# The front of the two routed feed-forward layers: fewer identity products, statistics first, a third chunk copied inside the attention step, more tiles normalised on ScalarE

## The reference, cut to what matters

```python
x = x + 0.5 * L0_ffn(layernorm(x))   # 8 experts, the best 2 of a softmax gate, and a shared expert with a sigmoid gate
x = x + L0_attn(layernorm(x))        # 16 heads of width 8, 4 key heads
x = x + 0.5 * L0_ffn(layernorm(x))
x = x + 0.5 * L1_ffn(layernorm(x))   # 8 zones, 3 of them by the pooled sequence
x = x + L1_attn(layernorm(x))
x = x + 0.5 * L1_ffn(layernorm(x))
```

```python
logits = x_flat @ gate_w.T
scores = softmax(logits)
_, topk_ids = lax.top_k(scores, 2)
w = scores * one_hot(topk_ids, 8).sum(axis=1)
```

## Time and profile before

| what | value |
|---|---|
| runs, median of 3 | 1454.32 us (1452.37 to 1456.07) |
| the profiled execution, its own time | 1451.83 us |
| its span | 1450.0 us |
| TensorE busy | 1394.0 us, 96% of the span |
| VectorE, ScalarE, GpSimd busy | 1129.6, 976.5, 640.3 us |
| first expert product of stage 0 | 38.9 us after the start |
| first expert product of stage 2 | 619.7 us after the start |

### The profile page before, as it was taken

The page is one execution under the profiler, slowest core; times in us unless marked ns, Lnnn a source line. Parts: engine busy times, 40 slices in busy tenths (PEclk is TensorE's granted clock), DMA queues, the critical chain, the costliest instruction groups (busy, mean ns, idle before and its releaser), DMA issues.

```text
span 1450.0 us, 26990 instructions
## 1 busy us (share of the span) xinstructions
PE 1394.0 (96%) x9348; PEld 1116.9 (77%) x9348; DVE 1129.6 (78%) x2503; ACT 976.5 (67%) x1759; POOL 640.3 (44%) x600
## 2 busy tenths in 40 slices
PE   6999999999999999999999999999989999989998
PEld 6788888766666665678888878999967777769998
DVE  6787777688988889678777787787788889855765
ACT  5666666557777777766666668877656666658886
POOL 6466666610000000146666667677512323356664
PEclk9999999999999999999999999999999999989999
DMA  6000000000000000002000011000000000000001
GB/s 184 1 1 1 1 1 1 1 1 1 1 1 1 1 1 2 1 1 90 1 1 1 1 38 51 1 2 2 1 1 2 1 2 2 2 1 2 15 16 30
DMA packets 13318, 16.84 MB, mean 12 GB/s; under 512 B 768, under 2 KB 10496, under 8 KB 12928
## 3 DMA queue, kind: packets, MB, share of 16 engines
q1 hardware_dynamic: 13184, 15.11, 3.4%
HBM read 13.01 MB, written 2.10 MB: 10 GB/s over the span
## 4 chain that ended last, share of the span: by engine, by line
PE 82%; DVE 10%; issue 3%; ACT 2%; POOL 2%; DMA 0%; POOLq 0%; SPq 0%; DVEq 0%; ACTq 0%
PE PS L852 19%; PE PS L879 9%; PE PS L2073 9%; PE PS L2090 8%; PE PS L1017 5%; PE PS L1037 5%; PE PS L1025 4%; PE PS L996 2%; PE PS L1414 2%; PE PS L1439 2%; PE PS L1448 2%; PE PS L1424 1%; PE PS L170 1%; PE PS L1472 1%; PE PS L1396 1%
## 5 line engine op out<-in xcount | busy, mean ns | idle before, releaser
L759 POOL TENSOR_TENSOR RR<-AR,RR 128x512 fp32r<-128x512 f32 x150 | 193.9, 1293 | 139.4 <-ACT RR L784 133.0
L823 ACT ACTIVATE AR<-PS 128x512 f32<-128x512 f32 x224 | 134.0, 598 | 148.4 <-PE PS L852 144.7
L724 DVE TENSOR_TENSOR AR<-AR,PS 128x512 f32<-128x512 f32 x224 | 153.4, 685 | 101.4 <-PE PS L852 90.3
L1142 ACT ACTIVATE AR<-PS 128x512 f32<-128x512 f32 x256 | 152.5, 604 | 85.6 <-PE PS L1025 84.8
L1222 DVE TENSOR_REDUCE AR<-PS 128x2 f32<-128x512 f32 x256 | 172.5, 687 | 21.5 <-PE PS L1017 20.6
L852 PE MATMUL PS<-XHI,WG 128*128 128x512 f32 x448 | 178.7, 399 | 0.4 <-DVE XLO L459 0.3
L852 PE MATMUL PS<-XHI,WU 128*128 128x512 f32 x448 | 175.0, 391 | 2.0 <-DVE AR L724 2.0
L730 DVE TENSOR_TENSOR AR<-AR,PS 128x512 f32<-128x512 f32 x224 | 154.0, 687 | 9.4 <-PE PS L868 1.3
L2345 POOL CAST SL<-ZW 128x1024 fp32r x96 | 100.3, 1045 | 84.3 <-PE PS L2090 83.8
L2073 PE MATMUL PS<-XHI,SL 128*128 128x256 f32 x576 | 134.1, 288 | 2.2 <-DVE XTR L2240 1.9
L2168 ACT ACTIVATE PS<-PS 128x1024 f32<-128x1024 f32 x96 | 96.9, 1009 | 58.1 <-PE PS L2073 57.8
(11 more groups left out here) (299 smaller groups left out, 3598.8 us busy)
## 6 DMA issues: line engine op xcount, KB each, us to landing
X<-in_x SPq DMA_DIRECT2D x4, 512.0 KB, 6.5
out_x<-X SPq DMA_DIRECT2D x4, 512.0 KB, 3.2
AR<-in_w SPq DMA_DIRECT2D x1, 1792.0 KB, 12.0
XT<-in_w SPq DMA_DIRECT2D x1, 1608.0 KB, 6.5
AR<-in_zone_up SPq DMA_DIRECT2D x6, 256.0 KB, 5.3
AR<-in_zone_down SPq DMA_DIRECT2D x6, 256.0 KB, 5.7
XT<-in_sel SPq DMA_DIRECT2D x1, 896.0 KB, 7.0
SM<-in_small SPq DMA_DIRECT2D x1, 857.5 KB, 7.0
```

What stands on the lines that cost most here:

```text
L724: v.tensor_tensor(PRD[:, m % 2, :], SIL[:, m % 2, :], bank(2 + m % 2), ALU.mult).then_inc(S.prod, 1)
L759: g.tensor_tensor(HL[k % 3], GAT[:, m % 2, :], HH[k % 3].bitcast(F32), ALU.subtract).then_inc(S.h_lo, 1)
L823: act.activation(SIL[:, m % 2, :], bank(m % 2), ACT.Silu).then_inc(S.silu, 1)
L1142: act.activation(PT[:, g % 2, k, 2 * jp:2 * jp + 2, :], bank(2 + m % 2).rearrange("p (j q) -> p j q", j=2), ACT.Exp, scale=SC0).then_inc(S ...
```

## The change

Five things are done:

1. stage 0 issues 6 identity products ahead of its first transposes in place of 20;
2. stage 0 does `x_stats(3)` and `stats_in(0, 1)` ahead of chunk 0 on VectorE, and `root_in(0, 1)` and `scale_in(0, 1)` in the pass of chunk 0 in place of that of chunk 1;
3. the last attention step also does chunk 2 of stage 2: `copies_in(2)` and `normed_in(4)` at m = 10 on ScalarE, `low(2)`, `normed_dve(4)` and `logits_out(1)` at m = 11 on VectorE, and the loops of stage 2 start at chunk 3;
4. `gate_logits` of stage 2 goes right behind `stats_in(2, 1)`, ahead of `low(3)`;
5. in stage 2 ScalarE normalises 3 tiles of each of chunks 4 to 7 in place of 2, and VectorE 1 in place of 2.

```diff
@@ on_act
-            return TPC if n == 0 else 0 if c < AHEAD else TPC // 2
+            return TPC if n == 0 else 0 if c < AHEAD else 2 if c < 4 else 3
@@ f0_norm_dve
                 stats_in(n, 0)
                 scale_in(n, 0)
                 x_stats(2)
+                x_stats(3)
+                stats_in(n, 1)
             else:
                 stats_in(n, 1)
             gates = Chain(v, S.gate_chain, D.gate_chain)
-            for c in range(AHEAD if n else 0, NC):
+            if n:
+                gate_logits(v, n, gates, 0)
+            for c in range(3 if n else 0, NC):
                 if n == 0:
                     copy_in(n, c)
                 low(n, c)
-                if n == 0 and c == 0:
-                    x_stats(3)
-                if n == 0 and c == 1:
-                    stats_in(n, 1)
-                    scale_in(n, 1)
-                if n and c == NC - 3:
+                if n == 0 and c == 0 or n and c == NC - 3:
                     scale_in(n, 1)
                 if c + 2 < NC:
                     normed_dve(n, c + 2)
                 if c > 0:
                     logits_out(n, c - 1)
-                if c == 2:
+                if n == 0 and c == 2:
                     gate_logits(v, n, gates, 0)
@@ f0_norm_pe
-                keep_busy(pe, bank(3), 20)
+                keep_busy(pe, bank(3), 6)
@@ f0_norm_act
-            for c in range(AHEAD if n else 0, NC):
+            for c in range(3 if n else 0, NC):
                 copies_in(n, c)
                 if c == 3:
                     gate_exps(n, 0)
+                if n == 0 and c == 0:
+                    root_in(n, 1)
                 if c + 2 < NC:
                     normed_in(n, c + 2)
-                if n == 0 and c == 1:
-                    root_in(n, 1)
@@ a0_act, step
+                    if i == NB and m == 10:
+                        copies_in(n + 1, 2)
+                        normed_in(n + 1, 4)
@@ a0_dve, step
+                    if i == NB and m == 11:
+                        low(n + 1, 2)
+                        normed_dve(n + 1, 4)
+                        logits_out(n + 1, 1)
```

## The result

The changed kernel takes 1447.02 us (median of 7 runs, 1443.71 to 1448.68) against 1455.44 us (1451.72 to 1457.54) for the kernel before: a ratio of 0.9942, 95% interval 0.9927 to 0.9958, or 8.4 us. The forecast was 6.0 us. Its profiled execution has a span of 1446.1 us, 3.9 us less than that of before, so the profile shows less than half of what the medians show. The other half goes with a higher mean clock of TensorE in the runs, and was not in the forecast.

What follows compares the result with a forecast made beforehand. TensorE, busy 96% of the span, was taken as the bound, with waits in the fronts of stages 0 and 2. 6.2 - 0.2 = 6.0 us off the median gave 1448.3; own range 1445.4 to 1450.8, with rivals to 1452.3.

Steps and rivals of the forecast that it cites:

- the main part: Stage 0 front: fewer identity products and earlier statistics bring the first expert product from 38.93 to 32.7, 6.2 us earlier.
- Six products, statistics first: Stage 0: transposes at 12.5, second root about 15.45, then ScalarE takes 2.02 us a chunk; first expert product at 31.7.
- nothing taken off: Stage 0 before the two 0.5 us deductions: chunk 3's high part at 21.1, first expert product at 31.7.
- term b: Stage 0: TensorE may reach the fast pace later than 14.5, delaying chunk 2's transposes; 0.5 us taken, between nothing and 0.6.
- rival A: Stage 0 clock: fast pace only at 21 to 25, first expert product 33.6 to 35.0, gain 4 to 5, 1449.8; chance 0.12.
- term a: Stage 0 gate_logits: line 537, with both inputs in SBUF, meets GpSimd's subtractions on the path; 0.5 us taken, between nothing and 1.0.
- the 10.6 us that the sum kept: Stage 0: the stretch from chunk 3's high part to the first expert product (38.93 - 28.31) keeps its old order and length.
- rival C: Stage 0: gate-weight lines 590 to 594 wait for GpSimd's down-weight subtractions, up to 2 us late; 1450.0; chance 0.13.
- Passed through: After stage 0's first expert product the order is unchanged, so the whole shift reaches stage 2's first transposes.
- Stage 2 (a loss of 0.2): Stage 2 front: chunk 6's high part and low(6) come 0.1 to 0.2 us later; loss of 0.2, 0.5 either side.
- nothing takes this up: Stage 2: chunk 4's transposes start at 609.3 instead of 610.96, but ScalarE's copy of chunk 4 stays near 612.4 (was 612.5).

Runs made afterwards that it cites:

- changed again: The changed kernel run once more with nothing altered, beside the later kernels: 1446.13 us, 9.6 us below the kernel before.
- 2 tiles: The changed kernel with ScalarE normalising 2 tiles instead of 3 in chunks 4 to 7 of stage 2: 1446.14 us (median of four runs).
- before again: The kernel before run once more, unaltered, for a second trace; mean clock 0.990. Medians of the kernel before in the three groups: 1456.71, 1455.98, 1455.76 us.

## Why the prediction was right, point by point

The forecast was 1448.3 us in a range of 1445.4 to 1452.3; measured 1447.02. The mechanism of the main part was right: the statistics first remove ScalarE's wait, and the shift is passed through. The closeness of the number is in part luck. The two fronts of the profile gave 4.8 us and not 6.0, about 4 us came with a higher clock that the sum didn't have, and the seven runs of before have a median 1.1 us above the three that the sum was taken from.

- **Six products, statistics first.** Transposes at 12.5 (12.52), high part of chunk 0 at 14.1 (13.91), root at 15.2 (15.17), high part of chunk 3 at 21.1 with nothing taken off: 20.94 to 21.07 in the five traces whose fast pace came by 17. The first expert product was worked out at 31.7 with nothing taken off; 31.36 to 31.50 in those. The cadence of ScalarE as what decides this front is shown. In the first trace of the changed kernel itself chunk 3's high part came at 22.99 and the first expert product at 33.43, outside the 21 to 22 and 32 to 33 that the prediction gave as signs. The shares of the two edits don't add up: the statistics alone bring the first expert product to 32.90, the products alone to 38.72 (with the fall of 10 us), both to 31.5.
- **The slow pace (term b, 0.5 us).** Too small for the two traces of the changed kernel: 1.9 and 3.8 us of delay (33.43 and 35.33 against 31.5), and nothing in others. I had bounded it by 0.6, taking a rise at 18.2 as the latest. The prediction's rival A has about the right price (35.0 for a rise at 25, measured 35.33). Its sign, the slow pace for more than a chunk after 18, came in both traces of the changed kernel (to about 21 and 25), two of the five with 6 products and both edits, so 0.12 was too small a chance.
- **Line 537 (term a, 0.5).** It took 0.23 us in both traces of the changed kernel and 0.56 to 0.73 in five others, but 0.55 in before too, inside the 10.6 us that the sum kept. And it isn't on the path: ScalarE loads a table for 1.28 us ahead of the exponents, and line 537 ends before that load does. The kernel with 12 products, VectorE (there it is line 536) and then ScalarE:

```profile
21.35 0.63 DVE L536 TENSOR_TENSOR PS<-AR 128x64 f32<-128x64 f32 x1
```

```profile
21.67 1.28 ACT L543 ACT_TABLE_LOAD   x1
```

  From chunk 3's high part to the first expert product it is 10.42 to 10.46 us in all eight traces with the statistics first, whether line 537 took 0.23 or 0.73. The term should have been nothing.
- **The gate's weights (rival C).** It came true at the side of the forecast and not in place of it: 0.4 us (changed again) to 1.65 us (2 tiles) between the first expert product and `up(0, 1)`, over the 3.08 of before. (A loss of 2 us off 6.0 makes 1450.3, where the prediction has 1450.0.) I had argued that one input in SBUF keeps an operation out of GpSimd's way. The Trainium skill (SBUF — State Buffer, "Who interferes with whom") has copies and `tensor_scalar` among those that can take the shared port pair, and the traces agree with it and not with my argument: 0.16 us for the add from PSUM, 0.99 from SBUF.
- **Passed through.** 559.8 us between the fronts in both.
- **Stage 2 (a loss of 0.2).** Wrong in sign: a gain of 0.37 us, in four traces alike (17.49 or 17.50). The third tile was priced right: 0.44 us on ScalarE less 0.3 on VectorE, measured 0.16 net. What failed is "nothing takes this up": with 2 tiles the moved chunk and the earlier gate logits bring the exponents 0.53 us forward, counted from the first transposes (605.03 - 595.90 = 9.13, before 611.52 - 601.86 = 9.66), and the front keeps all of it (17.87 to 17.34).
- **What was left out.** The sum was made against one profiled execution with a mean clock of 0.992, while the median execution of before has 0.989 to 0.990 and pays for falls after its holes: 3.0 us in stage 0 in the second trace. I saw the fall at 28.4 and took it as hidden, which it is but for 0.2 us at its length there, and not at three times that (3.1 us). The change removes the hole. Windows over whole traces show the low level between 25 and 38 in each of the five traces with the old statistics and the hole left as it was (3.4 us in three, 10.2 in two), and in none of the other nine (eight with the statistics first, one with the hole filled). At half clock such a fall takes 0.0012 or 0.0035 off a mean over 1450 us (an estimate: 1.7 / 1450 and 5.1 / 1450), while the medians differ by 0.004 to 0.006. So the hole is a shown source of a part of the other 4 us, and not of all; in the five traces it cost 0.2 us three times and 3.1 to 3.5 twice, and filling it alone gave 1.6 us in the ratio, with nothing in the interval. The falls at 599 to 628, 870 to 894 and 1274 to 1296 occur in traces of old and new kernels both. Whether the change makes them rarer, or the rest is chance, would need many traces of each kernel, and stays open.

## What to carry to other kernels

Ask of every engine in a start-up chain what it waits for and whether that work could be done while another transfer is still on its way: eight statistics moved from between two chunks to ahead of the first were worth more than all the rest here. Price a hole of TensorE not by its length but with the low clock behind it, and look at the mean clock of several runs before a profiled execution is taken as the typical one. Small VectorE adds and copies from SBUF to SBUF that run beside a long GpSimd instruction can wait for its end; here, moving their input to PSUM took the wait away and cost nothing that the traces show. And before a slower instruction is put into a sum, look whether another engine's work already covers it, as the table load did.

## What the runs showed that I had not expected

- A hole of 4.1 us was followed by 3.1 us of the low level in one trace of the kernel before, a hole of 4.7 us by 10 us in the other; with the hole filled there was none.
- The low level lasted through full work of TensorE: 14.00 us of 14.00 busy at 0.51 in the front of stage 2 of "before again".
- The granted clock reads 1.00 at the start of every trace, while the pace of the transposes (1.06 us for four, 0.60 later) shows the lower level until 12 to 25 us.
- Of three VectorE operations on 8 elements in a row beside GpSimd, the add of a constant and the copy waited up to 0.8 us each, the reciprocal between them never (0.20 us from SBUF in each trace).
